# One core, two attention and two expert layers: new engine orders, fillers tied to the next step's PSUM bank, and scatters issued without spacers

## The chip, the cores and the metric

One core of one Trainium2 chip runs the whole program in one launch. The metric is the device time of that execution in microseconds. The engines are TensorE (PE), VectorE (DVE), ScalarE (ACT), GpSimd (POOL) and SyncE (SP, here only a DMA queue).

## What is computed

Input `x` is [2, 512, 128], the context is [2, 77, 128]. Four residual blocks follow each other:

```python
x = x + attn0(layernorm(x), ctx)      # 16 heads of 8, softmax over 77 keys, scores*tau + delta
x = x + ffn0(layernorm(x))            # top-1 of 8 experts picks a rank-4 LoRA on a shared 128->512->128 relu FFN
x = x + attn1(layernorm(x), ctx)
x = x + moe(layernorm(x))             # top-1 of 8 experts, 128->512->128 with gelu, times the top probability
```

## The kernel before

Two batches (b = 0, 1) of 512 rows, each as four 128-row tiles, pass through all four blocks. Every engine walks a list of steps written out by hand in `TABLES` (line 69 on); an entry such as `sc/1/0/5:7` is kind / layer / batch / index. All waiting between engines is by semaphores, so a table fixes only the order inside one engine. `banks()` walks PE's list and deals the steps that write a shared PSUM bank round-robin to four banks; `hold(key)` makes PE wait until the previous step in the same bank has been read.

The kinds that matter here: `xt` transposes the normalised rows, `q` and `kp` and `vp` are projections, `max` and `mt` find a score bound for each query and put it in the query operand, `sc` and `pv` are scores and the product with the values, `rd` and `on` the normalisation of the attention output, `wo` and `out` close a block, `gate` / `ut` / `hid` are the LoRA FFN.

The last block sorts rows by expert. `route/b` and `rank/b` compute a slot for each row. `row/b/0` to `row/b/3` are four indirect DMAs of POOL (line 556) that scatter 128 rows each to `slots` in DRAM. When all four have landed, SP loads `XS` back in four pieces (line 456). There are 11 tiles of 128 slots for each batch, 22 in all. For tile n, `m1/n-1` and `m1/n` on PE hold one transpose of tile n (line 1112) and the first product (line 1119); ACT applies gelu (line 690); `m2/n` is the second product (line 1131); DVE copies the expert's weights (`cw`, line 892), adds a bias (`bs`, line 900) and closes the tile (`m2`, line 905); POOL makes the bias product (`pb/n`, line 517) and sends the tile to the output by an indirect DMA (`so/n`, line 566). `ln/3/1` on POOL is the root of the last layer norm of batch 1 (line 525): DVE's `xn/3/1` waits for it, and so do `xt/3/1`, `route/1`, `rank/1` and `row/1`.

Two kinds of padding exist. `busy` steps are PE matmuls of a constant 128x512 bf16 tile into an `acc` bank that nobody reads at that time (line 924): 9 before the first step, then 5+5+5+1+1+1+4 in the first 20 us, then 8 before `wo/1/1`. `gap` steps are POOL memsets of three columns, each followed by a wait for its own end (line 559): 15 of them, wherever two indirect DMAs of POOL would follow each other directly (three among `row/0`, six from `row/1/0` to `so/4`, and six later). Where a `pb` stands between two `so`, there is none.

Of the kernel before, what the change touches and what calls it, by code (L numbers as in the profile page):

```python
# [67 lines left out]

TABLES = {
    "pe": """  # L70
        kp/0 xt/0/0 vp/0 busy/0/5 q/0/0/0:2 busy/0/5 max/0/0/0:3 busy/0/5 max/0/0/3:5 busy/0/1 max/0/0/5 busy/0/1
        max/0/0/6 busy/0/1 max/0/0/7 busy/0/4 mt/0/0/0 max/0/0/8 xt/0/1 max/0/0/9:11 sc/0/0/0:2 max/0/0/11:13
        q/0/1/0 sc/0/0/2:4 max/0/0/13:15 pv/0/0/0:2 max/0/0/15 max/0/1/0 sc/0/0/4 pv/0/0/2 mt/0/0/1 max/0/1/1:3
        pv/0/0/3 max/0/1/3 sc/0/0/5 max/0/1/4 pv/0/0/4 sc/0/0/6:8 max/0/1/5:7 q/0/1/1 pv/0/0/5 max/0/1/7 sc/0/0/8
        pv/0/0/6 mt/0/1/0 sc/0/0/9 max/0/1/8 pv/0/0/7:9 sc/0/1/0 max/0/1/9 pv/0/0/9 max/0/1/10:14 sc/0/1/1 pv/0/1/0
# [20 lines left out]
    "dve": """
        ln/0/0 xn/0/0 kp/0 ln/0/1 ks/0 vp/0 km/0/0 q/0/0/0:2 max/0/0/0:8 xn/0/1 mt/0/0/0 max/0/0/8:13 q/0/1/0
        max/0/0/13:16 max/0/1/0 mt/0/0/1 max/0/1/1:8 q/0/1/1 max/0/1/8 mt/0/1/0 on/0/0/0 max/0/1/9:13 on/0/0/1
        max/0/1/13:16 wo/0/0 ln/1/0 mt/0/1/1 xn/1/0 gate/0 ut/0 hid/0/1 ks/1 on/0/1/0 hid/0/3 on/0/1/1 out/0 ln/2/0
        wo/0/1 xn/2/0 ln/1/1 xn/1/1 vp/1 q/1/0/0 max/1/0/0:4 gate/1 max/1/0/4:7 ut/1 max/1/0/7 q/1/0/1 hid/1/1  # L100
        max/1/0/8 mt/1/0/0 hid/1/3 max/1/0/9:12 out/1 max/1/0/12 ln/2/1 max/1/0/13:16 xn/2/1 mt/1/0/1 q/1/1/0
        max/1/1/0:8 on/1/0/0 mt/1/1/0 on/1/0/1 q/1/1/1 wo/1/0 ln/3/0 max/1/1/8:10 xn/3/0 max/1/1/10:16 route/0
# [12 lines left out]
}
# [1118 lines left out]
```

## Time and profile before

| | us |
|---|---|
| median of 3 runs | 199.19 (198.74 to 200.07) |
| the profiled execution, its own time | 199.31 |
| its span in the profile | 197.5 |
| PE busy | 164.6 (83%) |
| DVE busy | 122.7 (62%) |
| ACT busy | 98.1 (50%) |
| POOL busy | 79.7 (40%) |

The span starts with the first instruction recorded and ends with the last event; 1.81 us of the device time lie around it. Busy is the sum of the engine's instruction records. The mean granted TensorE clock was 0.918 of full.

### The profile page before, as it was taken

What the parts mean: (1) busy time and instruction counts of PE and PEld (TensorE: products, weight loads), DVE (VectorE), ACT (ScalarE), POOL (GpSimd) and SP (SyncE); (2) the same over time, 40 slices, a digit from 0 to 9 for tenths busy, and PEclk for the clock granted to TensorE, in tenths of its full rate; (3) what the DMA queues carried; (4) which work ended last, traced back from release to release, by engine and by line L of the source; (5) the groups of instructions that cost most, each with busy time, mean ns of one, the idle gap of its engine ahead of it and who ended that gap; (6) DMA issues with size and microseconds to landing.
All of it is one profiled execution on the core that took longest, in us unless ns stands there. A gap on an engine that the chain in (4) does not pass through costs nothing. (4 is left out here: it accounts for less than half of the span.)

```text
span 197.5 us, 3411 instructions
## 1 busy us (share of the span) xinstructions
PE 164.6 (83%) x879; PEld 117.9 (60%) x879; DVE 122.7 (62%) x359; ACT 98.1 (50%) x230; POOL 79.7 (40%) x110
## 2 busy tenths in 40 slices
PE   7678999999998587999998999908899769999500
PEld 2424665667557446468554665408889769999400
DVE  2899885894664797574669985543778617543100
ACT  5374657865731330442596636603477637666200
POOL 8898600004050540000200003617376678887751
PEclk9999999999999655599999999975999999999965
DMA  6400003400000000002999900137001281000100
GB/s 184 160 2 3 6 3 84 166 0 2 3 0 0 0 2 3 5 3 33 278 400 490 352 9 25 61 83 241 4 14 67 70 267 39 16 7 8 35 9 0
DMA packets 14483, 15.48 MB, mean 78 GB/s; under 512 B 6842, under 2 KB 11205, under 8 KB 14400
## 3 DMA queue, kind: packets, MB, share of 16 engines
q1 hardware_dynamic: 12944, 13.29, 21.1%
q0 software_dynamic: 1088, 1.60, 2.5%
q10 hardware_dynamic: 432, 0.37, 0.7%
q8 instruction: 8, 0.13, 0.3%
q14 instruction: 11, 0.09, 0.2%
HBM read 13.50 MB, written 5.44 MB: 96 GB/s over the span
## 5 line engine op out<-in xcount | busy, mean ns | idle before, releaser
L1029 PE MATMUL acc<-P,VP 123*128 123x512 f32 (+1 forms) x80 | 39.3, 593 | 0.0
L690 ACT ACTIVATE HT<-scores,B 128x128 f32<-128x128 f32 x88 | 25.2, 371 | 14.0 <-PE scores L1119 11.1
L547 POOL TENSOR_TENSOR X<-X,ROWS 128x512 f32<-128x512 f32 x6 | 7.6, 1272 | 55.6 <-DVE XN L732 55.5
L780 DVE TENSOR_REDUCE MR<-shared 128x4 f32<-128x308 f32 x64 | 26.6, 470 | 3.9 <-PE shared L989 3.4
L644 ACT ACTIVATE P<-scores 123x512 f32<-123x512 f32 (+1 forms) x40 | 22.9, 595 | 12.3 <-PE scores L1014 11.6
L566 POOL DMA_INDIRECT out<-XS,token x22 | 22.5, 1021 | 12.2 <-POOL XN L559 7.2
L1131 PE MATMUL acc<-W,HT 128*128 x176 | 23.1, 278 | 2.3 <-ACT HT L690 2.3
L1119 PE MATMUL scores<-XST,HT 128*128 128x128 f32 x176 | 24.8, 288 | 0.0
L989 PE MATMUL shared<-KG,QG 98*128 98x308 f32 x64 | 22.5, 415 | 1.1 <-DVE QG L770 0.8
L1119 PEld LDWEIGHTS scores<-XST,HT 128*128 128x128 f32 x176 | 22.9, 203 | 0.0
L1131 PEld LDWEIGHTS acc<-W,HT 128*128 128x128 f32 x176 | 21.1, 192 | 2.9 <-issue 2.9
L1014 PE MATMUL scores<-QG,KG 102*123 102x512 f32 (+1 forms) x48 | 22.4, 520 | 0.0
L556 POOL DMA_INDIRECT slots<-ROW,slot x8 | 8.2, 1031 | 29.4 <-issue 24.7
L1029 PEld LDWEIGHTS acc<-P,VP 123*128 123x128 f32 (+1 forms) x80 | 14.2, 190 | 7.4 <-issue 6.1
L892 DVE COPY HT<-W 128x512 f32 x22 | 12.6, 571 | 8.1 <-issue 5.3
L989 PEld LDWEIGHTS shared<-KG,QG 98*128 98x128 f32 x64 | 12.4, 206 | 7.7 <-DVE QG L770 3.2
L629 ACT ACTIVATE QG<-shared,ATT 64x512 fp32r<-64x512 f32 x16 | 10.9, 684 | 11.9 <-PE shared L971 11.6
L770 DVE SCALAR_TENSOR_TENSOR QG<-shared,ATT,QG 32x512 fp32r<-32x512 f32 x16 | 11.9, 745 | 5.4 <-ACT QG L629 5.0
L1112 PE MATMUL shared<-CON,XS 128*128 128x128 f32 x22 | 6.9, 312 | 8.4 <-DMA XS<-slots 8.3
L1014 PEld LDWEIGHTS scores<-QG,KG 102*123 102x123 f32 (+1 forms) x48 | 8.6, 185 | 8.1 <-issue 4.8
L924 PE MATMUL acc<-idle 128*128 128x512 bf16 x39 | 11.4, 427 | 1.6 <-DVE idle L705 1.5
L905 DVE SCALAR_TENSOR_TENSOR XS<-acc,XS 128x128 f32<-128x128 f32 x22 | 7.4, 344 | 8.4 <-PE acc L1131 8.0
(122 smaller groups left out, 257.3 us busy)
## 6 DMA issues: line engine op xcount, KB each, us to landing
W<-in_w SPq DMA_DIRECT2D x16, 256.0 KB, 7.2
slots<-in_empty SPq DMA_DIRECT2D x1, 2860.0 KB, 14.8
XS<-slots SPq DMA_DIRECT2D x2, 650.0 KB, 5.8
XS<-slots SPq DMA_DIRECT2D x2, 390.0 KB, 3.9
W<-in_ffn0w SPq DMA_DIRECT2D x1, 534.0 KB, 4.8
XS<-slots SPq DMA_DIRECT2D x2, 260.0 KB, 2.8
X<-in_x SPq DMA_DIRECT2D x2, 256.0 KB, 4.3
B<-in_b SPq DMA_DIRECT2D x1, 512.0 KB, 5.4
```

Source lines behind the costliest of these rows:

```text
L566: pool.indirect_dma_start(out, bass.IndirectOffsetOnAxis(ap=token[:, t:t + 1], axis=0), XS[:, t, 0:D], None, bounds_check=B * S - 1, oob_i ...
L644: act.activation(P[0:w, n % NP], scores[n % 2][0:w, :], ACT.Exp).then_inc(probs_ready, 1)
L690: ins = act.activation(HG1[:, t % NHB, c], hidden[t % 2][:, c], ACT.Gelu_apprx_tanh, bias=B1[:, bass.ds(expert[t] * NF + k, 1)])
L770: dve.scalar_tensor_tensor(QG[64:96, b, g], bank(s)[64 * odd:64 * odd + 32, :], ATT[l][0:32, A_BQ + g:A_BQ + g + 1], QG[0:32, b, g].bitcas ...
L780: dve.tensor_reduce(MR[:, b, qt, g, 2:2 + HG], bank(s)[:, 0:GK].rearrange("p (h k) -> p h k", h=HG), AX.X, ALU.max).then_inc(max_read, 1)
L892: dve.tensor_copy(W1C[:, n % NWC], W1[:, bass.ds(e * F, F)]).then_inc(w1_ready, 1)
L924: pe.matmul(unread[:, :], idle[:, 0:128], idle[:, 0:S], start=True, stop=True)
L989: pe.matmul(bank(s)[:, 0:GK], QG[0:ONES + 2, b, g, 128 * qt:128 * qt + 128], KG[0:ONES + 2, b, g, off:off + GK], start=True, stop=True).th ...
L1014: ins = pe.matmul(scores[n % 2][0:w, :], KG[:, b, g, c:c + w], QG[:, b, g], start=(i == 0), stop=(i == len(parts) - 1))
L1029: pe.matmul(acc[half][:, :], VP[0:w, l, b, j, half], P[0:w, n % NP, :], start=(j == 0), stop=(j == NT - 1)).then_inc(probs_used, 1)
L1119: ins = pe.matmul(hidden[t % 2][:, 128 * k:128 * (k + 1)], W1C[:, t % NWC, 128 * k:128 * (k + 1)], XST[:, t % 2], start=True, stop=True)
L1131: ins = pe.matmul(acc[n % 2][:, 0:D], HG1[:, n % NHB, 128 * k:128 * (k + 1)], W2[:, bass.ds(expert[n] * (NF * D) + D * k, D)], start=(k == ...
```

## The change

- `busy` steps are gone from PE's list. A dictionary `FILL` gives a number of the same filler matmuls to 14 steps, and `hold()` issues them after its wait for the bank and writes them into the step's own bank. In `q` and in those `max` steps that begin a head group, `hold` comes after the wait for the input; in `mt`, `wo`, `xt` and `ut` it comes before that wait.
- All four tables are in a new order (the diff is cut, and its long lines are wrapped). Among the moves: `vp/0` before `xt/0/0` on PE; `out/0` before `pv/0/1/9` and `vp/1` before `wo/0/1`; on DVE `vp/0` before `ks/0` and `vp/1` before `on/0/1/1`; `wo/1/0` after `mt/1/1/0` on PE; `m2/20` after `m1/21`.
- On POOL `ln/3/1` stands before `pb/0`, `pb/0` to `pb/7` before `so/0`, and all 15 `gap` steps are gone.

```diff
 TABLES["pe"]
-        kp/0 xt/0/0 vp/0 busy/0/5 q/0/0/0:2 busy/0/5 max/0/0/0:3 busy/0/5 max/0/0/3:5 busy/0/1 max/0/0/5 busy/0/1
+        kp/0 vp/0 xt/0/0 q/0/0/0:2 max/0/0/0:8 mt/0/0/0 max/0/0/8 xt/0/1 max/0/0/9 sc/0/0/0:2 max/0/0/10:13 q/0/1/0
...
-        pv/0/1/5 sc/0/1/7 pv/0/1/6 sc/0/1/8 ut/0 sc/0/1/9 pv/0/1/7 hid/0/0:4 pv/0/1/8:10 out/0 wo/0/1 xt/2/0 vp/1
+        pv/0/1/5:7 ut/0 sc/0/1/8 pv/0/1/7 hid/0/0:4 sc/0/1/9 pv/0/1/8 out/0 pv/0/1/9 vp/1 wo/0/1 xt/2/0 q/1/0/0
...
-        sc/1/1/9 pv/1/1/7:10 busy/1/8 wo/1/1 m1/-1:2 xt/3/1 m2/0 route/1 m2/1 m1/2 rank/1 m1/3 m2/2 m1/4 m2/3 m1/5
+        pv/1/1/7:10 wo/1/1 m1/-1:2 xt/3/1 m2/0 route/1 m2/1 m1/2 rank/1 m1/3 m2/2 m1/4 m2/3 m1/5:7 m2/4:6 m1/7 m2/6
...
-        m2/14 m1/17 m2/15:17 m1/18:20 m2/17 m1/20 m2/18:21 m1/21 m2/21
+        m1/19 m2/18 m1/20 m2/19 m1/21 m2/20:22
 TABLES["dve"]
-        mt/1/1/1 rank/0 tiles/0 cw/0:2 on/1/1/0 cw/2 on/1/1/1 cw/3 wo/1/1 ln/3/1 xn/3/1 cw/4:6 bs/0 m2/0 bs/1:3
-        route/1 m2/1 rank/1 cw/6 m2/2 cw/7 bs/3 cw/8 bs/4:7 cw/9 tiles/1 m2/3 bs/7 cw/10 bs/8 cw/11 m2/4:6 bs/9
+        mt/1/1/1 route/0 rank/0 tiles/0 cw/0:2 on/1/1/0:2 cw/2 wo/1/1 ln/3/1 xn/3/1 cw/3:5 bs/0:3 m2/0 route/1 m2/1
+        rank/1 bs/3 cw/5 bs/4 cw/6 m2/2 cw/7 m2/3 cw/8 bs/5:7 m2/4 tiles/1 bs/7 cw/9 m2/5 bs/8 cw/10 bs/9 m2/6 bs/10
 TABLES["pool"]
-        row/0/2 gap/2 row/0/3 pb/0 ln/3/1 pb/1:6 so/0 pb/6:8 so/1 pb/8:11 row/1/0 gap/3 row/1/1 gap/4 row/1/2 gap/5
-        row/1/3 gap/6 so/2 gap/7 so/3 gap/8 so/4 pb/11 so/5 pb/12 so/6 pb/13 so/7 pb/14 so/8 pb/15 so/9 pb/16 so/10
+        row/0/2 row/0/3 ln/3/1 pb/0:8 so/0 pb/8:10 so/1 pb/10 row/1/0 row/1/1 row/1/2 row/1/3 so/2 so/3 so/4 so/5
+        pb/11 so/6 pb/12 so/7 pb/13 so/8 pb/14 so/9 pb/15 so/10
...
+FILL = {('q', 0, 0, 0): 6, ('max', 0, 0, 0): 5, ('max', 0, 0, 3): 5, ('max', 0, 0, 4): 1, ('max', 0, 0, 5): 1, ('max',
+        0, 0, 6): 1, ('mt', 0, 0, 0): 5, ('wo', 0, 1): 7, ('q', 1, 0, 0): 3, ('xt', 1, 1): 5, ('max', 1, 0, 2): 1,
+        ('ut', 1): 7, ('wo', 1, 0): 2, ('wo', 1, 1): 9}
...
-                elif s[0] == "gap":
-                    finish(pool.memset(XN[:, 0, 0:3], 0.0), spaced)
...
             def hold(key):
 
                 if key in before:
                     wait_reader(before[key])
+                keep_busy(FILL.get(key, 0), bank(key))
...
-                elif kind == "busy":
-                    _, late, n = s
-                    if late:
-                        pe.wait_ge(on_ready, 2 * 2 * B - 1)
-                    keep_busy(n, acc[1 - late])
```

## Rows read from the trace of the kernel before

**Rows 1.** The page's 40 slices of 4.94 us: granted TensorE clock in tenths.

```profile
PEclk9999999999999655599999999975999999999965
```

**Rows 2.** The chain of work that ended last: start us, us, what.

```profile
128.58 2.43 DMA slots<-ROW,slot
...
156.19 3.42 DMA XS<-slots
...
192.48 0.97 POOL out L566
```

**Rows 3.** Windows: stretch, length, busy of PE, PEld, DVE, ACT, POOL, clock, DMA, GB/s.

```profile
66.40:83.40 17.00, 14.91 (x42) 9.61 (x42) 13.05 (x36) 5.01 (x9) 4.97 (x4) 0.51 0.05 3
...
133.20:156.80 23.60, 22.16 (x172) 20.95 (x172) 16.09 (x59) 14.14 (x52) 14.70 (x23) 0.91 0.23 76
...
159.60:184.20 24.60, 24.51 (x211) 23.90 (x211) 11.67 (x36) 14.73 (x55) 20.10 (x28) 1.00 0.19 60
```

**Rows 4.** Timeline near 10 to 16 us: start us, us, engine line, operation [idle before].

```profile
10.52 1.96 PE L971 MATMUL shared<-XNT,ATT 128*128 128x512 f32 x4 [0.53 <-issue]
12.32 1.24 PE L924 MATMUL acc<-idle 128*128 128x512 bf16 x5
...
13.36 3.08 DVE L770 SCALAR_TENSOR_TENSOR QG<-shared,ATT,QG 32x512 fp32r<-32x512 f32 x4
```

**Rows 5.** Timeline of PE from 66 to 85 us.

```profile
66.46 1.09 PE L938 MATMUL shared<-CON,XN 128*128 128x128 f32 x4 [3.19 <-DVE XN L732]
...
84.29 0.80 PE L1066 MATMUL shared<-U,LS 96*128 96x512 f32 x1
```

**Rows 6.** PE groups by form, 66.4 to 83 us and 83.5 to 110 us.

```profile
L971 PE MATMUL shared<-XNT,ATT 128*128 128x512 f32 x4 | 4.0, 1093 | 0.0
...
L971 PE MATMUL shared<-XNT,ATT 128*128 128x512 f32 x4 | 2.0, 593 | 0.0
```

**Rows 7.** Timeline of POOL: the scatters, a spacer, a bias product.

```profile
121.37 1.22 POOL L556 DMA_INDIRECT slots<-ROW,slot  x1 [23.80 <-issue]
...
127.19 0.61 POOL L559 MEMSET XN<- 128x384 f32 x1
128.58 0.97 POOL L556 DMA_INDIRECT slots<-ROW,slot  x1 [0.78 <-POOL XN L559]
...
146.43 1.04 POOL L556 DMA_INDIRECT slots<-ROW,slot  x1 [0.88 <-issue]
...
153.62 1.06 POOL L556 DMA_INDIRECT slots<-ROW,slot  x1 [0.78 <-DVE XS L905]
...
162.07 1.04 POOL L566 DMA_INDIRECT out<-XS,token  x1 [0.17 <-issue]
163.14 0.41 POOL L517 TENSOR_TENSOR PB<-B,XS 128x128 f32<-128x128 f32 x1
163.71 1.04 POOL L566 DMA_INDIRECT out<-XS,token  x1 [0.17 <-issue]
...
191.25 0.44 POOL L559 MEMSET XN<- 128x384 f32 x1
```

**Rows 8.** Timeline of the last block: the root's chain, first transposes, the last tile.

```profile
130.39 0.17 DVE L720 TENSOR_SCALAR var_eps<-mean_var 128x4 f32<-128x4 f32 x1
...
134.59 1.05 POOL L525 TENSOR_TENSOR rstd<-var_eps,mhalf 128x4 f32<-128x4 f32 x1
...
133.25 0.48 PE L1112 MATMUL shared<-CON,XS 128*128 128x128 f32 x1 [5.01 <-DMA XS<-slots]
...
137.90 0.60 PE L938 MATMUL shared<-CON,ROW 128*128 128x128 f32 x4
...
159.65 0.33 PE L1112 MATMUL shared<-CON,XS 128*128 128x128 f32 x1 [2.80 <-DMA XS<-slots]
...
185.58 1.15 PE L1131 MATMUL acc<-W,HT 128*128 x8 [1.42 <-ACT HT L690]
...
186.84 0.35 DVE L905 SCALAR_TENSOR_TENSOR XS<-acc,XS 128x128 f32<-128x128 f32 x1 [2.81 <-PE acc L1131]
```

More of the change, by code:

```diff
@@ L70 @@
     "pe": """
-        kp/0 xt/0/0 vp/0 busy/0/5 q/0/0/0:2 busy/0/5 max/0/0/0:3 busy/0/5 max/0/0/3:5 busy/0/1 max/0/0/5 busy/0/1
[L72 to L75, printed above, removed]
@@ L76 @@
-        sc/0/1/2 max/0/1/14:16 sc/0/1/3 wo/0/0 sc/0/1/4 mt/0/1/1 pv/0/1/1:5 sc/0/1/5 xt/1/0 kp/1 gate/0 sc/0/1/6
-        pv/0/1/5 sc/0/1/7 pv/0/1/6 sc/0/1/8 ut/0 sc/0/1/9 pv/0/1/7 hid/0/0:4 pv/0/1/8:10 out/0 wo/0/1 xt/2/0 vp/1
-        q/1/0/0 xt/1/1 max/1/0/0:4 gate/1 max/1/0/4:7 ut/1 max/1/0/7 q/1/0/1 hid/1/0:3 max/1/0/8 mt/1/0/0 hid/1/3
-        sc/1/0/0:2 max/1/0/9:12 out/1 sc/1/0/2 max/1/0/12:14 pv/1/0/0 sc/1/0/3 max/1/0/14 pv/1/0/1 max/1/0/15
-        pv/1/0/2 sc/1/0/4 mt/1/0/1 pv/1/0/3 xt/2/1 pv/1/0/4 sc/1/0/5:7 q/1/1/0 sc/1/0/7 pv/1/0/5:7 max/1/1/0
@@ L86 @@
-        m2/14 m1/17 m2/15:17 m1/18:20 m2/17 m1/20 m2/18:21 m1/21 m2/21
+        kp/0 vp/0 xt/0/0 q/0/0/0:2 max/0/0/0:8 mt/0/0/0 max/0/0/8 xt/0/1 max/0/0/9 sc/0/0/0:2 max/0/0/10:13 q/0/1/0
+        max/0/0/13 sc/0/0/2:4 max/0/0/14:16 pv/0/0/0:3 mt/0/0/1 max/0/1/0:3 sc/0/0/4 pv/0/0/3 max/0/1/3 sc/0/0/5
+        pv/0/0/4 sc/0/0/6:8 max/0/1/4:6 pv/0/0/5 max/0/1/6:8 q/0/1/1 pv/0/0/6 sc/0/0/8 mt/0/1/0 pv/0/0/7 max/0/1/8
+        sc/0/0/9 pv/0/0/8 max/0/1/9 sc/0/1/0 pv/0/0/9 max/0/1/10:12 sc/0/1/1 max/0/1/12 sc/0/1/2 max/0/1/13 pv/0/1/0
@@ new lines @@
+        max/0/1/14:16 wo/0/0 sc/0/1/3:5 mt/0/1/1 pv/0/1/1:3 kp/1 sc/0/1/5:7 xt/1/0 pv/0/1/3 gate/0 pv/0/1/4 sc/0/1/7
+        pv/0/1/5:7 ut/0 sc/0/1/8 pv/0/1/7 hid/0/0:4 sc/0/1/9 pv/0/1/8 out/0 pv/0/1/9 vp/1 wo/0/1 xt/2/0 q/1/0/0
+        xt/1/1 max/1/0/0:4 gate/1 max/1/0/4:7 ut/1 max/1/0/7 q/1/0/1 hid/1/0:3 max/1/0/8 mt/1/0/0 hid/1/3 sc/1/0/0
+        max/1/0/9:11 sc/1/0/1 max/1/0/11 out/1 max/1/0/12 sc/1/0/2 max/1/0/13 pv/1/0/0:2 sc/1/0/3 max/1/0/14:16
+        pv/1/0/2 sc/1/0/4 xt/2/1 pv/1/0/3 mt/1/0/1 q/1/1/0 pv/1/0/4 sc/1/0/5:7 q/1/1/1 max/1/1/0:2 sc/1/0/7 pv/1/0/5
@@ new lines @@
+        sc/1/0/8 max/1/1/2 pv/1/0/6 sc/1/0/9 max/1/1/3:7 pv/1/0/7 max/1/1/7 pv/1/0/8 max/1/1/8 pv/1/0/9 max/1/1/9:13
+        mt/1/1/0 max/1/1/13 wo/1/0 sc/1/1/0 max/1/1/14 sc/1/1/1 pv/1/1/0 sc/1/1/2:4 pv/1/1/1 max/1/1/15 xt/3/0
+        mt/1/1/1 route/0 pv/1/1/2 rank/0 sc/1/1/4 pv/1/1/3 sc/1/1/5:7 pv/1/1/4 sc/1/1/7 pv/1/1/5:7 sc/1/1/8:10
+        pv/1/1/7:10 wo/1/1 m1/-1:2 xt/3/1 m2/0 route/1 m2/1 m1/2 rank/1 m1/3 m2/2 m1/4 m2/3 m1/5:7 m2/4:6 m1/7 m2/6
+        m1/8:10 m2/7:9 m1/10 m2/9 m1/11 m2/10 m1/12:14 m2/11 m1/14 m2/12 m1/15 m2/13 m1/16:18 m2/14 m1/18 m2/15:18
@@ L93 @@
-        q/1/1/0 sc/1/0/7 rd/1/0/0 sc/1/0/8:10 rd/1/0/1 q/1/1/1 mt/1/1/0 sc/1/1/0:2 ln/3/0 sc/1/1/2:4 xt/3/0 mt/1/1/1
-        route/0 sc/1/1/4:10 rd/1/1/0:2 m1/-1:1 xt/3/1 m1/1 route/1 m1/2:22
+        ln/0/0 ks/0 xt/0/0 ln/0/1 q/0/0/0:2 mt/0/0/0 xt/0/1 sc/0/0/0:2 q/0/1/0 sc/0/0/2:4 mt/0/0/1 sc/0/0/4:8
+        rd/0/0/0 q/0/1/1 sc/0/0/8 mt/0/1/0 sc/0/0/9 sc/0/1/0 rd/0/0/1 sc/0/1/1:4 mt/0/1/1 ln/1/0 sc/0/1/4 xt/1/0
+        sc/0/1/5 kp/1 sc/0/1/6 ks/1 sc/0/1/7:9 hid/0/0 rd/0/1/0 hid/0/2 sc/0/1/9 rd/0/1/1 ln/2/0 xt/2/0 ln/1/1
@@ L95 @@
+        q/1/0/0 xt/1/1 q/1/0/1 hid/1/0 hid/1/2 mt/1/0/0 sc/1/0/0:3 ln/2/1 sc/1/0/3 xt/2/1 sc/1/0/4 mt/1/0/1 q/1/1/0
+        sc/1/0/5:7 q/1/1/1 sc/1/0/7:10 rd/1/0/0:2 mt/1/1/0 sc/1/1/0:2 ln/3/0 sc/1/1/2 xt/3/0 sc/1/1/3 route/0
+        mt/1/1/1 sc/1/1/4:8 rd/1/1/0 sc/1/1/8:10 rd/1/1/1 m1/-1:1 xt/3/1 m1/1 route/1 m1/2:22
     """,
     "dve": """
-        ln/0/0 xn/0/0 kp/0 ln/0/1 ks/0 vp/0 km/0/0 q/0/0/0:2 max/0/0/0:8 xn/0/1 mt/0/0/0 max/0/0/8:13 q/0/1/0
-        max/0/0/13:16 max/0/1/0 mt/0/0/1 max/0/1/1:8 q/0/1/1 max/0/1/8 mt/0/1/0 on/0/0/0 max/0/1/9:13 on/0/0/1
@@ L99 @@
[L99 to L102, printed above, removed]
-        mt/1/1/1 rank/0 tiles/0 cw/0:2 on/1/1/0 cw/2 on/1/1/1 cw/3 wo/1/1 ln/3/1 xn/3/1 cw/4:6 bs/0 m2/0 bs/1:3
@@ L104 @@
-        route/1 m2/1 rank/1 cw/6 m2/2 cw/7 bs/3 cw/8 bs/4:7 cw/9 tiles/1 m2/3 bs/7 cw/10 bs/8 cw/11 m2/4:6 bs/9
-        cw/12:14 m2/6:8 bs/10:13 m2/8 cw/14 m2/9 cw/15:17 bs/13 m2/10 bs/14 cw/17:19 m2/11 cw/19 m2/12 bs/15 m2/13
-        bs/16 m2/14 cw/20 bs/17:19 cw/21 m2/15:19 bs/19:21 m2/19 bs/21 m2/20:22
+        ln/0/0 xn/0/0 kp/0 ln/0/1 vp/0 ks/0 km/0/0 q/0/0/0:2 max/0/0/0:8 xn/0/1 mt/0/0/0 max/0/0/8:14 q/0/1/0
+        max/0/0/14:16 mt/0/0/1 max/0/1/0:8 q/0/1/1 mt/0/1/0 on/0/0/0 max/0/1/8:13 on/0/0/1 max/0/1/13:16 wo/0/0
@@ new lines @@
+        ln/1/0 mt/0/1/1 xn/1/0 gate/0 ut/0 ks/1 hid/0/1 hid/0/3 on/0/1/0 out/0 ln/2/0 vp/1 on/0/1/1 xn/2/0 wo/0/1
+        ln/1/1 xn/1/1 q/1/0/0 max/1/0/0:4 gate/1 max/1/0/4:7 ut/1 max/1/0/7 q/1/0/1 hid/1/1 max/1/0/8 mt/1/0/0
+        hid/1/3 max/1/0/9:12 out/1 ln/2/1 max/1/0/12 xn/2/1 max/1/0/13:16 mt/1/0/1 q/1/1/0 max/1/1/0:2 q/1/1/1
+        max/1/1/2:7 on/1/0/0 max/1/1/7:12 on/1/0/1 max/1/1/12 mt/1/1/0 wo/1/0 ln/3/0 max/1/1/13 xn/3/0 max/1/1/14:16
+        mt/1/1/1 route/0 rank/0 tiles/0 cw/0:2 on/1/1/0:2 cw/2 wo/1/1 ln/3/1 xn/3/1 cw/3:5 bs/0:3 m2/0 route/1 m2/1
@@ L107 @@
+        rank/1 bs/3 cw/5 bs/4 cw/6 m2/2 cw/7 m2/3 cw/8 bs/5:7 m2/4 tiles/1 bs/7 cw/9 m2/5 bs/8 cw/10 bs/9 m2/6 bs/10
+        cw/11 m2/7:10 cw/12 bs/11 cw/13 m2/10 cw/14:16 bs/12 cw/16 m2/11 cw/17 bs/13 cw/18 bs/14 m2/12:14 cw/19
+        bs/15 m2/14 bs/16 cw/20 bs/17 m2/15 bs/18 m2/16 cw/21 m2/17 bs/19:21 m2/18:20 bs/21 m2/20:22
     """,
     "pool": """
-        one/0 pre/0/0 km/0/1 pre/0/1 one/1 pre/1/0 km/1/0 pre/2/0 km/1/1 pre/1/1 pre/2/1 row/0/0 gap/0 row/0/1 gap/1
-        row/0/2 gap/2 row/0/3 pb/0 ln/3/1 pb/1:6 so/0 pb/6:8 so/1 pb/8:11 row/1/0 gap/3 row/1/1 gap/4 row/1/2 gap/5
@@ L111 @@
-        row/1/3 gap/6 so/2 gap/7 so/3 gap/8 so/4 pb/11 so/5 pb/12 so/6 pb/13 so/7 pb/14 so/8 pb/15 so/9 pb/16 so/10
-        gap/9 so/11 pb/17 so/12 pb/18 so/13 gap/10 so/14 pb/19 so/15 pb/20 so/16 pb/21 so/17 gap/11 so/18 gap/12
-        so/19 gap/13 so/20 gap/14 so/21
-    """,
-}
+        one/0 pre/0/0 km/0/1 pre/0/1 one/1 pre/1/0 km/1/0 pre/2/0 km/1/1 pre/1/1 pre/2/1 row/0/0 row/0/1 row/0/2 row/0/3 ln/3/1 pb/0:8 so/0 pb/8:10 so/1 pb/10 row/1/0 row/1/1 row/1/2 row/1/3 so/2 so/3 so/4 so/5 pb/11 so/6 pb/12 so/7 pb/13 so/8 pb/14 so/9 pb/15 so/10
@@ L368, in build @@
         z_ready = sem("z_ready")
-        spaced = sem("spaced")
         stored = sem("stored")
@@ L924, in keep_busy, with hold @@
                     pe.matmul(unread[:, :], idle[:, 0:128], idle[:, 0:S], start=True, stop=True)
+            def hold(key):
+                if key in before:
+                    wait_reader(before[key])
+                keep_busy(FILL.get(key, 0), bank(key))
             pe.wait_ge(idle_ready, 1)
```

13 lines of the change are left out of this document (2 added, 11 removed).

## The prediction

> **What bounds the kernel now.** The chain of waits comes first [rows 2]. It begins at 128.58 with the landing of the last row scatter of batch 0, passes through the load of `XS` for batch 1, which lands at 159.60, and ends in POOL's last output scatter at 192.48. So the last block is bound in turn by scatters, by PE, and by POOL. Next the stages [rows 3]. From 159.6 to 184.2 PE is busy 24.51 of 24.60 us: there PE is the bound. Before 133.25 PE waits for the scatters of batch 0 and their load, 5.01 us in one piece, and before 159.65 for those of batch 1, 2.80 us [rows 8]. At the end the last tile is closed on DVE at 187.19 [rows 8], and the last scatter begins only 5.29 us later [rows 2]: there POOL is the bound, because it works through its list at a fixed pace. Last the clock [rows 1]: it is full but for 64 to 84 us, the turn from batch 0 to the next things at 130 to 137, and the end. The long stretch is granted 0.51, that is 1.2 GHz, from 66.4 to 83.4 [rows 3]; PE had stood idle for 3.19 us before it [rows 5].
>
> **The change, part by part.** All times are of the profiled execution (span 197.5, own time 199.31, which is 0.12 over the median of 199.19).
>
> Start. Five fillers took 1.24 us [rows 4], so one costs about 0.215 (the last record has a tail). Six now stand behind the wait for the transposed rows and in front of the first `q`: q comes 1.3 us later than 10.52. DVE takes the q results only from 13.36, since it is busy with keys until then, and so most of this is covered: ACT's two halves of 0.7 each put the first DVE half at about 13.7. Five fillers in front of `max/0/0/3` now wait for DVE's last q, which costs 0.2 more. I take +0.5. If the clock fell in the 2 us in which PE now stands idle before `q`, it would be +2. At best it is -0.4, by the V product that has moved into an idle place. `vp/0` earlier on DVE starts SP's 24 small transfers of V 1.4 us sooner, which nobody waits for.
>
> Clock from 66 to 84. `wo/0/1` gets 7 fillers ahead of its wait for `on`, `out/0` now runs before the last `pv`, and `vp/1` fills the rest. PE's idle of 3.19 us shrinks to pieces of under 1 us. `q/1/0/0`, `xt/1/1` and `ut/1` get 3, 5 and 7 for the next gaps. A q matmul record is 1093 ns in the slow stretch and 593 behind it [rows 6]. What this is worth is bounded by DVE, which has 13.05 us of work in those 17.00 [rows 3]: at most 4.0 us, at least 0 if the clock falls all the same. Followed: xt/2/0 is not earlier (66.4); the batch 1 rows of the norm are 0.8 later since `wo/0/1` on DVE now waits behind `xn/2/0`, and DVE's q stands at 71.0; `gate/1`, for which DVE waited at 75.3, comes 1.2 earlier; the second q on PE takes 1.0 instead of 1.9 and three `hid` steps 3.4 instead of 4.6. The last of these, at 84.3 to 85.1 [rows 5], comes 3.3 earlier. Behind it PE is full until 106 (the slices of the profile and the window from 83.4 on show no gap), so it carries on. I take -3.3. The fillers there are 23 x 0.215 = 4.9 us of PE, inside waits; only the 3 before `q/1/0/0` are behind its input, 0.65 us, counted above. The many other swaps of `max`, `sc`, `pv` between 20 and 60 and between 85 and 121 keep the same instructions on a full PE: 0, between -1 and +1. Weights and the empty slots are loaded some 6 us sooner; they were not waited for.
>
> So the first row scatter moves from 121.37 [rows 7] to 121.37 + 0.5 - 3.3 = 118.6.
>
> Scatters of batch 0. With spacers: 121.37 to 129.55, that is 8.18 for four. A spacer costs its 0.44 or 0.61 and the 0.78 behind it, since POOL waits for its end and only then sets up the next DMA: 2.2 or 2.36 from scatter to scatter [rows 7]. No row shows two scatters in direct succession. From below: the record of 1.02 and the 0.17 that stands before a DMA whose setup is hidden, 1.19. From above: with nothing hidden, 0.97 + 0.79 = 1.76, and further up the pace with spacers. The nearest row is the pair with one product between, 1.64 from start to start [rows 7], and without its 0.41 it is 1.2. I take 1.19. Four then end at 118.6 + 4 x 1.02 + 3 x 0.17 = 123.2. The first transpose came 3.70 after the last scatter's end (129.55 to 133.25 [rows 8]): now 126.9. PE is done with `wo/1/1` (128.2 before) at 125.4, so it waits 1.5 us instead of 5.01, and the clock stays up.
>
> The root. `var_eps` was ready at 130.56 and the root ran at 134.59 to 135.64, behind the product that waits for the load [rows 8]. Now: 127.8 + 1.05, and `xn` 1.3 behind it, 130.2. `xt/3/1` stands behind two first products: it came 4.65 after the first transpose (133.25 to 137.90), at the low clock; at full clock 3.3, so 130.2 too. I take 130.3. From there to the first scatter of batch 1 it was 8.53 (137.90 to 146.43), made of DVE's chain of small operations, and stays: 138.8. Eight products now stand before `so/0`, 3.6 us from 129, over by 133: nobody waits. Four scatters end at 143.4 instead of 154.68. The load's landing and transpose followed 4.97 behind (to 159.65): 148.4.
>
> PE in batch 0. From 133.25 to 156.8 it needed 23.55, at a mean clock of 0.91 [rows 3]; at full clock 1.4 less, 22.15. From 126.9 this ends at 149.1. That is later than 148.4, so PE no longer waits for batch 1: the tile that began at 159.65 begins at 149.1.
>
> PE in batch 1. 159.65 to the close of the last tile at 187.19 is 27.54. `m2/20` now stands behind `m1/21` and fills 0.9 of the 1.42 us in which PE waited for the last gelu [rows 8]: 26.6, so the last tile is closed at 175.7. POOL must have kept up: from 143.4 it has 20 scatters x 1.19 + 11 products x 0.45 = 28.8, done at 172.2 if nothing came late. So it waits for DVE now. The last scatter starts 0.8 after the tile is closed (the setup behind a wait, as behind a spacer), takes 1.0, and the span ended 4.05 behind it (193.45 to 197.5): 181.6. With 1.81 around the span, 183.4.
>
> I add 1.1 for seams of a new order that no row shows (copies of weights on DVE now later against `m1`, scatters closer to DVE's copies): 184.5.
>
> A rule of the Trainium skill speaks against the largest term. DMA: Bandwidth & Descriptors, section on the anatomy of one DMA on the GpSimd path, gives each such DMA a fixed cost of about 2.0 us, with its data on top. If that were the pace of a queue of them, as an estimate 2.0 + 0.3 for 133 KB, the spacers would lie in time that is lost anyway and the sum would be near the second rival. The trace disagrees for the pace: 1.64 us from start to start [rows 7].
>
> **The rivals.**
> First, the clock falls all the same, or the setup is not hidden. A clock that falls at 66 gives back 3.3. With 1.76 per direct pair the first transpose is at 128.6, batch 1's load lands at 151.8, later than PE is done, and the sum grows by 2.7. Either alone is 187 to 188, both 190.5. For it: the idle of 2 us at the start is new, and 1.76 is what a spacer's wait leaves when the spacer is taken out. Against it: the setup is hidden behind a product.
> Second, a direct pair costs what a pair with a spacer costs, 2.2 or 2.36: POOL's own limit, which the spacer merely filled. Then only start and clock are left, 199.3 - 2.8 - 0.4 for the last tiles: 196.1.
> Third, the other side: a scatter that follows another directly is held until the first has landed. Landing took 1.46 behind the end of the record (2.43 in all [rows 2]), so a pair costs 0.97 + 1.46 + 0.79 = 3.2. Then the first transpose is at 132.9 at the low clock, `row/1/0` at 146.0, its fourth ends at 156.7, and POOL ends nine direct pairs x 3.2 and eleven others x 1.61 later, at 203.2: span 207.3, time 209. It is slower from a pair cost of 2.5 on: 15 pairs against 14.3 + 19.8 us of spaced pace and 3.2 of other gain. For it: the spacers stand exactly and only between direct neighbours, and no row shows direct neighbours. Against it: a product of 0.41 is no landing, and 1.64 is under 2.43, so POOL does not wait for landings in general.
>
> **How the numbers follow.** Forecast 0.63 (its own range 181 to 188), first rival 0.18 (187 to 192), second 0.07 (196), third 0.12 (200 to 209). The low end is the whole 4.0 of clock, no loss at the start, and no seams: 181. The range goes up to 196.5 and leaves out the third rival. A change of 1% is about what a measurement of this kernel can tell from none. Faster by over 1%: 0.63 + 0.18 + most of the second, 0.86. Within 1%: 0.03. Slower: 0.11.
>
> **What would show it.** Right: POOL's direct scatters 1.1 to 1.3 apart; the clock at 1.00 from 60 to 84; first transpose of the last block near 127 and no wait of PE for `XS` of batch 1; the last scatter starting under 1.2 us behind the last tile's close. Wrong: direct pairs over 1.8 apart, or idle of PE before 150 for the load, or a granted clock of 0.5 after 60.

## The result, and the profile after

The changed kernel takes 188.71 us (median of 4 runs, 187.45 to 189.88) against 199.41 for the kernel before beside it (198.74 to 200.07): a ratio of 0.9462, 95% interval 0.939 to 0.9534. The profiled execution took 189.11, its span 187.3, its mean clock 0.967. The forecast was 184.5.

In the page of the kernel after, the clock's slices are these. The long dip of [rows 1] is short now, and there is a new one in the third slice:

```profile
PEclk9969999999999999669999999999999999999997
```

Windows of the kernel after (stretch, length, busy of PE, PEld, DVE, ACT, POOL, clock, DMA, GB/s). The first answers to the clock's stretch of [rows 3], the other two to PE's two batches of the last block, tile 0 to tile 11 and tile 11 to the close of tile 21:

```profile
67.00:84.00 17.00, 13.61 (x56) 8.19 (x58) 12.61 (x38) 3.27 (x7) 4.98 (x4) 0.80 0.07 4
...
132.42:156.07 23.65, 21.18 (x181) 20.12 (x181) 16.52 (x70) 14.29 (x53) 16.05 (x22) 1.00 0.34 99
156.07:181.47 25.40, 24.43 (x213) 23.89 (x211) 13.44 (x39) 15.63 (x59) 20.08 (x26) 1.00 0.19 60
```

Timeline of POOL in the kernel after: the four scatters of batch 0 and the root, the first two scatters of batch 1, and the last scatter. These answer to [rows 7]:

```profile
123.73 1.23 POOL L555 DMA_INDIRECT slots<-ROW,slot  x1 [24.95 <-issue]
125.26 0.97 POOL L555 DMA_INDIRECT slots<-ROW,slot  x1 [0.30 <-issue]
126.53 0.98 POOL L555 DMA_INDIRECT slots<-ROW,slot  x1 [0.30 <-issue]
127.82 0.97 POOL L555 DMA_INDIRECT slots<-ROW,slot  x1 [0.30 <-issue]
134.04 1.05 POOL L524 TENSOR_TENSOR rstd<-var_eps,mhalf 128x4 f32<-128x4 f32 x1 [5.25 <-DVE var_eps L717]
...
145.16 1.07 POOL L555 DMA_INDIRECT slots<-ROW,slot  x1 [0.88 <-issue]
146.53 0.97 POOL L555 DMA_INDIRECT slots<-ROW,slot  x1 [0.30 <-DVE XS L902]
...
182.27 0.97 POOL L563 DMA_INDIRECT out<-XS,token  x1 [0.71 <-issue]
```

Within batch 0, from scatter to scatter it is 1.27 to 1.29 us, the record of 0.97 and an idle of 0.30, but for the first pair (1.53), whose first record is longer. In batch 1 the idle is 0.30 again and the pairs are 1.28 to 1.42 apart, since two records are longer. The four of batch 0 are over in 5.06 us, where they took 8.18. And the first scatter is late: 123.73, where [rows 7] have 121.37.

Timelines of PE and DVE in the kernel after, the ends of the last block, for [rows 8]:

```profile
132.42 0.33 PE L1105 MATMUL shared<-CON,XS 128*128 128x128 f32 x1 [0.79 <-DMA XS<-slots]
...
136.68 0.63 PE L936 MATMUL shared<-CON,ROW 128*128 128x128 f32 x4 [0.91 <-DVE ROW L729]
...
156.07 0.27 PE L1105 MATMUL shared<-CON,XS 128*128 128x128 f32 x1
...
179.86 1.15 PE L1124 MATMUL acc<-W,HT 128*128 x8 [0.52 <-ACT HT L687]
...
181.12 0.35 DVE L902 SCALAR_TENSOR_TENSOR XS<-acc,XS 128x128 f32<-128x128 f32 x1 [1.33 <-PE acc L1124]
```

The tile that waited 2.80 us for its load in the kernel before waits for nothing now (156.07), and the last scatter starts 0.80 after the last tile's close instead of 5.29.

The spans differ by 10.2: up to the first transpose 0.83 is gained (133.25 to 132.42), between the two batches' first tiles 2.75 (26.40 to 23.65), from there to the last close 2.14 (27.54 to 25.40), and behind it 4.48 (10.31 to 5.83). Up to the first scatter 2.36 is lost, so the last block, counted from there, gains 12.6 (a tail of 76.1 against 63.6).

### The profile page after: what moved, and what is told of

Its sections match the earlier page's. It is cut to its first block, busy times and chain, and to the rows that moved or that the text cites. A ratio compares the mean times of both kernels' runs of the same rounds, so it can differ in the third digit from the quotient of the medians.

```text
span 187.3 us, 3431 instructions
## 1 busy us (share of the span) xinstructions
PE 165.9 (89%) x902; PEld 115.9 (62%) x907; DVE 122.0 (65%) x359; ACT 97.4 (52%) x230; POOL 72.3 (39%) x95
## 4 chain that ended last, share of the span: by engine, by line
PE 61%; DVE 14%; issue 10%; POOL 5%; ACT 3%; DMA 2%; POOLq 1%; DVEq 0%; ACTq 0%
PE acc L1022 14%; PE scores L1112 7%; PE acc L1124 7%; PE scores L1007 5%; PE shared L1069 4%; PE shared L1055 4%; PE shared L982 4%; PE shared L964 3%; PE shared L916 3%; POOL out L563 3%; DVE QG L767 2%; DVE XN L729 2%; DVE MR L777 2%; DMA X<-in_x 2%; PE shared L1029 2%
## 5 line engine op out<-in xcount | busy, mean ns | idle before, releaser
L1022 PE MATMUL acc<-P,VP 123*128 123x512 f32 (+1 forms) x80 | 39.8, 595 | 0.4 <-ACT P L641 0.4
L1112 PE MATMUL scores<-XST,HT 128*128 128x128 f32 x176 | 23.3, 277 | 0.0
L1007 PE MATMUL scores<-QG,KG 102*123 102x512 f32 (+1 forms) x48 | 21.4, 503 | 0.1
L1112 PEld LDWEIGHTS scores<-XST,HT 128*128 128x128 f32 x176 | 21.4, 192 | 0.1
L916 PE MATMUL shared<-idle 128*128 128x512 bf16 x53 | 15.7, 421 | 5.8 <-ACT XNT L600 2.0
L889 DVE COPY HT<-W 128x512 f32 x22 | 11.0, 504 | 5.7 <-issue 4.7
L916 PEld LDWEIGHTS shared<-idle 128*128 128x128 bf16 x58 | 5.5, 103 | 14.4 <-issue 6.3
```

The lines of the kernel that those rows point to most:

```text
L889: dve.tensor_copy(W1C[:, n % NWC], W1[:, bass.ds(e * F, F)]).then_inc(w1_ready, 1)
L1007: ins = pe.matmul(scores[n % 2][0:w, :], KG[:, b, g, c:c + w], QG[:, b, g], start=(i == 0), stop=(i == len(parts) - 1))
L1022: pe.matmul(acc[half][:, :], VP[0:w, l, b, j, half], P[0:w, n % NP, :], start=(j == 0), stop=(j == NT - 1)).then_inc(probs_used, 1)
L1112: ins = pe.matmul(hidden[t % 2][:, 128 * k:128 * (k + 1)], W1C[:, t % NWC, 128 * k:128 * (k + 1)], XST[:, t % 2], start=True, stop=True)
```

## The experiments

All runs, with the own time of the profiled execution, the start of the first scatter (`row/0/0`) in it, and the tail from there to the end of the span:

| run | us, median | before, median | ratio (interval) | profiled | row/0/0 | tail |
|---|---|---|---|---|---|---|
| before | | 199.19 | | 199.31 | 121.37 | 76.1 |
| after | 188.71 | 199.41 | 0.9462 (0.939 to 0.9534) | 189.11 | 123.73 | 63.6 |
| e1 | 188.2 | 199.12 | 0.9449 (0.9387 to 0.951) | 185.61 | 119.96 | 63.8 |
| e2 | 199.35 | 199.12 | 0.9999 (0.9954 to 1.0044) | 200.54 | 123.31 | 75.4 |
| e3 | 186.25 | 199.12 | 0.9359 (0.929 to 0.9428) | 186.0 | 120.46 | 63.6 |
| e4 | 183.85 | 199.12 | 0.9244 (0.9171 to 0.9316) | 183.86 | 118.38 | 63.6 |
| e5 | 194.6 | 198.41 | 0.9754 (0.968 to 0.9829) | 194.59 | 123.14 | 69.7 |
| e6 | 196.13 | 198.41 | 0.9871 (0.9778 to 0.9964) | 196.29 | 122.70 | 70.6 |
| e7 | 195.39 | 198.41 | 0.9814 (0.9723 to 0.9906) | 193.92 | 121.52 | 70.5 |
| e8 | 193.66 | 198.41 | 0.976 (0.9677 to 0.9843) | 192.76 | 118.05 | 72.9 |
| e9 | 188.07 | 199.4 | 0.9446 (0.9414 to 0.9478) | 187.91 | 121.48 | 64.5 |
| e10 | 184.79 | 199.4 | 0.9297 (0.9229 to 0.9366) | 183.6 | 118.39 | 63.4 |
| e11 | 185.28 | 199.4 | 0.9313 (0.9241 to 0.9385) | 185.16 | 118.71 | 64.6 |
| e12 | 186.67 | 199.4 | 0.9342 (0.9252 to 0.9433) | 187.9 | 120.57 | 65.5 |

e1 to e4, e5 to e8 and e9 to e12 ran on three different chips. The kernel after itself ran in a set of its own, beside the kernel before only. The second set has long tails, which the third looks into; fronts can be compared across sets (e4 and e10, the same kernel, have 118.38 and 118.39). But one execution can differ from the next: the profiled execution of e1 is its shortest, 2.6 us under its median, and in e9, the same kernel, the front is 1.5 longer and the tail 0.7. The granted clock from 60 to 84 was 0.79 in the one and 0.72 in the other.

**e1, the spacers alone.** The kernel before without its 15 `gap` steps, all else as it was.

```diff
-        row/0/0 gap/0 row/0/1 gap/1 row/0/2 gap/2 row/0/3 pb/0 ln/3/1 pb/1:6 so/0 ...
+        row/0/0 row/0/1 row/0/2 row/0/3 pb/0 ln/3/1 pb/1:6 so/0 ...
```

> The kernel before with its 15 spacers taken out and nothing else. Theory A (the tail gains, the front of the new kernel loses): direct scatters 1.27 to 1.30 apart as in the changed kernel, first transpose of the last block about 3.2 earlier (130.1 instead of 133.25), the first scatter of batch 1 about 3 earlier, the last scatter under 1.2 behind the last tile's close: about 189 us, as fast as the whole change. Rival B (the orders and the root make the gain, the spacers were hidden): 195 to 199. The first row scatter stays at 121.4 under both.

188.2, the time of the whole change. Its tail is 63.8 where that of the change is 63.6. So the spacers explain the gain of the last block by themselves, and the gain of the whole change is no larger than theirs. The chain of work that ended last has these two pieces in e1 (start, us):

```profile
124.05 2.55 DMA slots<-ROW,slot
...
127.00 2.87 DMA XS<-slots
```

The last scatter lands 2.55 behind its start, and it started 1.28 behind its neighbour: these scatters do not wait for each other's landing. The DMA for a single scatter did not grow much either (2.43 in [rows 2]).

**e2, the change with spacers put back** at its 15 direct neighbours.

```diff
+        row/0/0 gap/0 row/0/1 gap/1 row/0/2 gap/2 row/0/3 ln/3/1 pb/0:8 ... gap/11 so/17 gap/12 so/18 ...
```

> The changed kernel with a spacer put back between every two POOL scatters that follow each other directly (15). Theory A: everything up to 123.7 stays, then scatters are 2.2 to 2.4 apart again, 3.3 later for the load of each batch and POOL is the bound at the end: 200 us or a little over, no faster than the kernel before. Rival B: the gain is kept, under 192.

199.35 against 199.12, with an interval of under half a per cent on both sides: nothing of the gain is left. Timeline of POOL in e2, a scatter, a spacer, a scatter:

```profile
125.97 0.97 POOL L554 DMA_INDIRECT slots<-ROW,slot  x1 [0.80 <-POOL XN L557]
126.94 0.44 POOL L557 MEMSET XN<- 128x384 f32 x1
128.16 0.97 POOL L554 DMA_INDIRECT slots<-ROW,slot  x1 [0.79 <-POOL XN L557]
```

2.19 apart, of which 0.44 is the memset and 0.79 the wait for its end and the setup behind it. A spacer so costs 0.92 against a direct pair of 1.27. A product of 0.41 that nobody waits for, in the spacer's place, makes mostly 1.57 to 1.65 (`so` steps; 1.64 in [rows 7]), so of the 0.92 about 0.6 is the wait and the rest the memset. No run had the memset without its wait. (The memset writes three tiles of 128 columns, not the three columns that the description of the kernel before gives it.)

**e3, without the 7 fillers of `ut/1`.** The question is where the front was lost.

```diff
-        ('ut', 1): 7, ('wo', 1, 0): 2, ('wo', 1, 1): 9}
+        ('wo', 1, 0): 2, ('wo', 1, 1): 9}
```

> The changed kernel without the 7 fillers at ut/1. They begin only when gate/1 is read, which is when ut's own input is ready, and ran at the low clock from 78.50 to 81.46. Theory A (they lie on the path): ut/1 starts about 2.9 earlier, near 78.6, and about that much reaches the end: 186. Rival C (PE is the bound behind it and takes the time back, or the clock stays low longer without them, up to 17 us of work at half speed as before): 188 to 191.

186.25, and row/0/0 at 120.46 instead of 123.73. In the kernel after, PE and DVE do this around `ut/1` (timelines):

```profile
77.76 0.69 DVE L825 TENSOR_TENSOR U<-shared,hot 128x128 f32<-128x128 f32 x3
...
78.50 0.61 PE L916 MATMUL shared<-idle 128*128 128x512 bf16 x1 [1.21 <-DVE U L825]
79.33 2.34 PE L916 MATMUL shared<-idle 128*128 128x512 bf16 x5 [0.22 <-DVE MR L777]
81.46 1.06 PE L1050 MATMUL shared<-CON,U 128*96 128x128 f32 x4
...
82.56 0.69 DVE L835 CAST U<-shared 96x512 fp32r<-96x512 f32 x1 [2.96 <-PE shared L1050]
```

The step before `ut/1` in its PSUM bank is `gate/1`, and what reads that bank last is DVE's `U` at 77.76, which is `ut/1`'s own input. So `hold`'s wait is over only when the step itself could start: no filler falls into the gap, all stand behind it, and they run while the clock is down (2.34 for five, where five take 1.24 in [rows 4]). DVE stands 2.96 us. From `xt/2/0` to `ut/1` it is 13.09 in the kernel after (68.37 to 81.46) and 10.13 in e3 (66.97 to 77.10).

Not all of these 2.96 us reach the end. In e3 the gap ahead of `ut/1` stays empty, and the clock is at 0.50 behind it, from 78 to 80. Timeline of PE in e3, `ut/1` and what follows:

```profile
77.10 0.73 PE L1050 MATMUL shared<-CON,U 128*96 128x128 f32 x4 [1.71 <-DVE U L825]
...
77.89 2.03 PE L964 MATMUL shared<-XNT,ATT 128*128 128x512 f32 x2
```

The q product takes 2.03 where the kernel after has 1.18. From `ut/1` to row/0/0 it is 43.36 in e3 and 42.27 in the kernel after. So the fillers behind their wait cost 2.96 and give back 1.09, a net loss of 1.87. The other 1.40 by which the fronts differ lies ahead of `xt/2/0`, where the code is the same; it is the clock at the start, looked at further down.

**e4, the same fillers ahead of the wait.** The 6, 5 and 7 of `q/0/0/0`, `max/0/0/0` and `ut/1` are issued before the step waits for anything, into an `acc` bank, and are taken out of `FILL`.

```diff
+EARLY = {('q', 0, 0, 0): 6, ('max', 0, 0, 0): 5, ('ut', 1): 7}
...
             for s in orders["pe"]:
                 kind = s[0]
+                keep_busy(EARLY.get(s, 0), acc[1])
```

> The changed kernel with the fillers of q/0/0/0 (6), max/0/0/0 (5) and ut/1 (7) moved in front of the step's first wait, into an accumulator bank that is free there; the same number of fillers. Theory A: the start gets 1.6 to 1.9 back (the clock no longer falls at 11.2, since PE is not idle from 8.4 to 10.45; first max reduction near 16.5 instead of 18.04), ut/1 gets 2.9 back: 184 to 185. Rival D (only the total number of fillers matters, not their side of the wait): 188 to 189.

183.85: 2.3% under e1 on the same chip (e10 and e9 below: 1.7%), and faster than either kernel of the case. The clock is full up to the last slice. Timeline of PE in e4, around the start and around `ut/1`:

```profile
8.35 1.46 PE L918 MATMUL acc<-idle 128*128 128x512 bf16 x6
10.46 1.95 PE L967 MATMUL shared<-XNT,ATT 128*128 128x512 f32 x4 [0.65 <-issue]
...
74.67 1.69 PE L918 MATMUL acc<-idle 128*128 128x512 bf16 x7
76.55 0.61 PE L1053 MATMUL shared<-CON,U 128*96 128x128 f32 x4 [0.19 <-DVE U L827]
```

Now the fillers lie in the gap, and `ut/1` starts 0.19 us after they end. row/0/0 is at 118.38; the forecast had 118.6.

**e5, only the start's fillers early; e6, no filler at all** in the new orders.

```diff
+EARLY = {('q', 0, 0, 0): 6, ('max', 0, 0, 0): 5}
```

> The changed kernel with only the fillers of q/0/0/0 (6) and max/0/0/0 (5) moved in front of the wait; ut/1 keeps its 7 behind. Theory: the idle of 2.04 us before q is filled, so the clock at the start is full in every run, first max reduction near 16.1 (as in the run with all three moved), and ut/1 still loses about 2.9 or what is left of it at full clock, 1.5: 186.5 to 188. If the start were worth nothing on the path: 188.7 as the changed kernel.

```diff
+FILL = {}
```

> The changed kernel's orders without any filler after the warm-up. Theory: the start has no filler on its path but its clock may fall (0 to +2), between 64 and 84 the clock falls once as in the kernel before and costs about 3, ut/1 gets its 2.9 back: 187 to 190. Rival: fillers bring nothing, since those ahead of a wait cost what they save: 186 or less.

By their fronts: in e5 DVE's first `max` reduction is at 16.10 (18.04 in the kernel after), but `xt/2/0` only 0.62 earlier (67.75), since the clock dipped between 16 and 40; `ut/1` with its fillers behind the input is at 81.09, and row/0/0 at 123.14. In e6 the clock is at 0.85 up to 16 and 0.81 from 16 to 40, and row/0/0 is at 122.70. So these executions show no gain of the front from the fillers as the change places them: without any it is 1.03 shorter than in the kernel after, and 0.44 shorter than in e5. That is less than the 1.40 that the clock of one execution makes, and the medians of the two point the other way (194.6 with the fillers, 196.13 without, intervals overlapping), so a small gain is not ruled out. Both missed their expectations, 186.5 to 188 and 187 to 190, and what their fronts and a tail of 63.6 make, 188 to 189.

**e7, the root alone; e8, early fillers alone**, both on e1's kernel, the old orders without spacers.

```diff
-        row/0/3 pb/0 ln/3/1 pb/1:6 so/0
+        row/0/3 ln/3/1 pb/0:6 so/0
```

> The kernel before without spacers and with the root ahead of the first bias product. Against the kernel before without spacers (188.2), where the root waited 1.0 us behind the product: theory (xt/3/1 stands behind two first products on PE and waits for them anyway, PE is the bound of batch 0): 187.5 to 188.5. Rival (root on the path): 187.2 or less.

```diff
+EARLY = {('xt', 2, 0): 14, ('q', 1, 0, 0): 2, ('xt', 1, 1): 8, ('ut', 1): 5}
```

> The kernel before without spacers, and with 14, 2, 8 and 5 fillers in front of the waits of xt/2/0, q/1/0/0, xt/1/1 and ut/1: old orders, clock kept. Theory: the clock stays at 1.00 from 60 to 84, hid/1 ends 3 to 4 earlier, first row scatter near 118, total 184 to 186, as fast as the new orders with their fillers ahead of the waits (183.85). Rival (the new orders make the front faster by themselves): 187 to 188.

Both missed what was expected (187.5 to 188.5, 184 to 186) and had tails of over 70 as well. As all four of this set had them, on one chip, with four different edits, the next set ran the kernels of e1, e4, e8 and e7 once more, together on another chip.

**e9 to e12, the kernels of e1, e4, e8 and e7 again.** No new edit.

> The kernel before less its 15 spacers, as measured once at 188.2 us. Theory 1 (the stalls of about 3 us each on waits from outside the core, seen in the second set of runs, belong to the chip of that set and not to its kernels): the time depends on this chip alone; on a chip like the first it is 188.2 again with a tail from the first scatter of row/0/0 to the end of the span of 63.8 us, on a chip like the second 195 with a tail of about 70. Theory 2 (they belong to those four kernels): 188.2 on any chip. Alone it decides only by reading 195; beside the next two runs it decides in either case.

> The kernel after with its early fillers ahead of the waits, as measured once at 183.85 us. Theory 1 (chip): tail equal to that of the run beside it within 0.5 us, so 183.9 where that one is 188.2, and 190 to 191 where that one is 195. Theory 2 (kernel): 183.9 on any chip.

> The kernel before less its spacers, with fillers ahead of four waits of batch 0, measured at 193.66 us in the second set. Theory 1 (chip): its front ended at 118.05 us, that of the run beside it at 119.96, so with equal tails it is 186.0 to 186.5 beside 188.2, and 193.5 beside 195. Theory 2 (kernel): 193.7 again with a tail of 72.9 us while the runs beside it keep 63.8.

> The kernel before less its spacers with the square root ahead of batch 0's last bias product, 195.39 us in the second set. Theory 1 (chip): within 0.7 us of the run without the root's move, 187.5 to 188.9 beside 188.2: the move saves at most the 1.15 us between var_eps and the root, and in the trace it moved nothing behind the scatters. Theory 2 (kernel): the root ahead of the product makes the stall on the scalar engine itself, and it is 195 beside 188.2.

The tails are 63.4 to 65.5 again, and the kernels of e7 and e8, unchanged, take 186.67 and 185.28 instead of 195.39 and 193.66. So the long tails come with the second set and not with these two kernels; e5 and e6 did not run again. That it is the chip, and not the time at which that set ran, is likely but not separated. Timelines of ACT and PE in e7:

```profile
145.69 0.28 ACT L679 ACTIVATE XST<-shared 128x128 f32<-128x128 f32 x1 [0.27 <-PE shared L1108]
149.45 1.14 ACT L686 ACTIVATE HT<-scores,B 128x128 f32<-128x128 f32 x4 [3.49 <-PE scores L1115]
151.02 0.28 ACT L679 ACTIVATE XST<-shared 128x128 f32<-128x128 f32 x1 [0.43 <-remote]
...
151.35 1.86 PE L1115 MATMUL scores<-XST,HT 128*128 128x128 f32 x8 [3.30 <-ACT XST L679]
```

and of ACT in e12, the same kernel:

```profile
145.31 0.29 ACT L679 ACTIVATE XST<-shared 128x128 f32<-128x128 f32 x1
146.19 1.14 ACT L686 ACTIVATE HT<-scores,B 128x128 f32<-128x128 f32 x4 [0.58 <-PE scores L1115]
```

Up to 146 the two agree within 0.4 us. Then ACT starts 3.26 us later than in e12 on a product that PE's records show as finished at the same time in both, DVE's next copy is late with it (149.46 against 146.20), PE runs dry behind them, and its clock falls (1.86 for eight, where e12 has 1.06). There is another such stall near the end (ACT waits 3.25 at 183.31). The profile names PE as the releaser of most of these waits and `remote`, a signal it can't place, for some. What makes them is open. So is why the kernel before shows nothing of them in its time (198.41), and whether direct scatters have a part in them, as all four kernels of the set had no spacers; that its last block had room in POOL's pace, 5.29 us at the end, is only argued. The kernel after itself was not run on that chip. e5, the nearest to it there, gained 2.5% and not 5.4%.

Within the third set the other questions have answers. Early fillers on the old orders give 185.28 against 188.07 (e11, e9), and the new orders with their own fillers, 18 of them early, 184.79 (e10): 0.5 less, well inside the intervals. The root's move (e12) reads 186.67 against 188.07, intervals overlapping; 187.5 to 188.9 was expected, and its four runs lie in two pairs, near 187.9 and 185.4. What the move does is seen better in e9 and e7, whose fronts end within 0.04 us of each other. Timeline of POOL in e9, the root and the first scatter of batch 1, and of PE, `xt/3/1`:

```profile
131.67 1.05 POOL L521 TENSOR_TENSOR rstd<-var_eps,mhalf 128x4 f32<-128x4 f32 x1
...
134.94 0.60 PE L934 MATMUL shared<-CON,ROW 128*128 128x128 f32 x4
...
143.46 1.05 POOL L552 DMA_INDIRECT slots<-ROW,slot  x1 [0.88 <-issue]
```

and in e7:

```profile
130.77 1.05 POOL L521 TENSOR_TENSOR rstd<-var_eps,mhalf 128x4 f32<-128x4 f32 x1 [4.07 <-DVE var_eps L716]
...
135.00 0.60 PE L934 MATMUL shared<-CON,ROW 128*128 128x128 f32 x4
...
143.52 1.05 POOL L552 DMA_INDIRECT slots<-ROW,slot  x1 [0.88 <-issue]
```

The root is 0.90 earlier and the scatter is not: `xt/3/1` stands on PE behind two tiles' first products, which wait for the load of `XS`, and the root was not what it waited for. But in both executions these products ran at a low clock (0.76 and 0.75 granted from 132 to 137). In e1 the clock stayed full there, and with the root still in its old place PE did wait for the normalised rows that hang on it. Timeline of PE in e1, `xt/3/1`:

```profile
132.64 0.63 PE L934 MATMUL shared<-CON,ROW 128*128 128x128 f32 x4 [0.49 <-DVE ROW L728]
```

So at full clock the move can be worth up to those 0.49 us, at the low clock nothing. No run shows the move alone at full clock.

## Why the prediction was off, step by step

The direction was right, and so was the largest cause, the spacers. The gain of 2.8 us that the front was to add did not come: the front lost 2.36. The forecast was 4.2 us under the median, and 188.71 lies outside the forecast's own band (181 to 188) and in that of the first rival (187 to 192); only the stated range, up to 196.5, takes it in. In the profiled execution it is 184.5 against 189.11, or 4.6: 5.1 too little up to row/0/0 and 0.6 too little behind it, less the 1.1 added for seams. Of the signs that were to show it right, the pace of most direct scatters and the last scatter's start came true. The clock from 60 to 84 did not (0.86), nor the first transpose near 127 (132.42), and a clock of 0.5 after 60, named as a sign of being wrong, is there.

**The start, +0.5 with +2 as the bound.** What the sum had wrong for this execution is that the clock would hold. PE stood idle for 2.04 us and the clock fell, to 0.50 from 12 to 14. Timeline of PE in the kernel after:

```profile
10.45 2.02 PE L916 MATMUL shared<-idle 128*128 128x512 bf16 x6 [2.04 <-ACT XNT L600]
12.26 3.06 PE L964 MATMUL shared<-XNT,ATT 128*128 128x512 f32 x4
```

and in e3, the same code with the clock full in the same place:

```profile
10.46 1.46 PE L916 MATMUL shared<-idle 128*128 128x512 bf16 x6 [2.04 <-ACT XNT L600]
11.75 1.88 PE L964 MATMUL shared<-XNT,ATT 128*128 128x512 f32 x4
```

The idle is the same, the clock is not. The first `max` reduction came at 16.64 in e3 and at 18.04 in the kernel after (16.47 before): +0.2 or +1.6, and `xt/2/0` at 66.97 or 68.37 (forecast 66.4, 66.46 before), that is +0.5 or +1.9. So "most of this is covered" holds at full clock, and both +0.5 and +2 were real. Which of them an execution gets is chance as far as these runs show, and the profiled one got the worse.

**The clock from 66 to 84, -3.3.** The step that failed is "the fillers there are inside waits; only the 3 before `q/1/0/0` are behind its input". The 7 of `ut/1` are behind it too. The term took the bank's wait to be over early, and it is over only when the step's own input is there. From `xt/2/0` to row/0/0 it is 55.36 in the kernel after, 54.91 before, and 51.96 in e4, where the fillers lie in the wait: -2.95 for the -3.3 that was forecast. What a kept clock is worth was right, and that this placement keeps it was wrong: of the fillers of `ut/1` alone, e3 and the kernel after make a net loss of 1.87.

**Scatters, 1.19 for a direct pair.** 1.27 to 1.29: the idle is 0.30 where 0.17 was taken from behind a product. With the longer first record of 1.23 the four make 5.06 instead of 4.6. The second rival (the pace of a spaced pair) and the third (a wait for the landing, 3.2) are out: e1 and e2 move the whole gain with the spacers, and no direct pair of row scatters in any run is over 1.54. In the first rival both halves had a part: the clock did fall in places, and the setup's cost is 0.30, between 0.17 and 0.79. From the end of the last scatter's record to the first transpose it was 3.63 for 3.70.

The Trainium skill, DMA: Bandwidth & Descriptors, section on the anatomy of one DMA on the GpSimd path, gives a fixed 2.0 us for each such DMA. The landings that the chains show, 2.43 and 2.52 from the start with spacers and 2.44 to 2.72 without, agree with it; the pace of 1.27 shows that this cost overlaps from one to the next. The Trainium skill, Perfetto Trace Analysis, section "DMA Instruction — SWDGE (GPSIMD)", says that the record of such a DMA ends when its descriptors are written, not when its data has moved. By that rule the next scatter may begin behind the record, and the trace agrees (0.97 of record, 0.30, the next).

**The root, 0.9 earlier for batch 1.** It is worth nothing at the low clock, as e7 and e9 show, and at most 0.49 at full clock by e1. In the new orders `var_eps` also came later: its record starts 10.05 behind row/0/0 (133.78) instead of 9.02, and 10.07 in e4, where e9 with the old orders has 8.98. It is batch 1's attention that ends later there: DVE's last `OT` starts 6.01 behind row/0/0 (129.74) instead of 4.91. From row/0/0 to row/1/0 it is 21.43 in the kernel after and in e4, 21.98 and 21.23 in e9 and e1; 20.2 was forecast. The step from `xt/3/1` to row/1/0 was 8.48 for 8.53.

**PE in batch 0, 22.15.** 23.65. The clock was full as forecast; PE was busy 21.18 and so idle for 2.47, 1.0 more than the 1.44 of [rows 3]; 0.91 of it lies ahead of `xt/3/1`, which came 4.26 behind the first transpose and not 3.3. That PE does not wait for batch 1's load was right.

**PE in batch 1, 26.6, and the end.** 25.40 and 5.83 (5.85 forecast): the first is 1.2 better than forecast, and `m2/21` waits 0.52 as worked out. POOL is no longer the bound at the end.

**Seams, +1.1.** There was no such loss: the tail from row/0/0 is 63.6 where the terms without seams made 63.0, and what was lost are the 0.46 of the scatters and the 1.5 less 1.2 on PE.

## What to carry to other kernels

A small instruction whose own end is waited for, between two indirect DMAs of one queue, costs about 0.9 us a time here (2.19 against 1.27), some 0.6 of it the wait, and it is worth its place only where a race or a landing asks for it. A filler fills a gap only where it is issued ahead of the wait that makes the gap: before it is put behind a bank's wait, look up who reads that bank, and whether the step itself waits for the same reader. If runs of one kernel come out some per cent apart from set to set while the kernel before stays, run the same kernels again, on another chip too, before explaining the difference.
